# First layer's variance: the squares of centred tokens, in place of the squares of x less the squared mean

## The chip, the core and the metric

The kernel runs on one core of one Trainium2 chip. A core has five engines with queues of their own, which meet only at semaphores: TensorE (PE in the profile; its weight loads are PEld), VectorE (DVE), ScalarE (ACT), GpSimd (POOL) and SyncE (SP), which here only issues transfers. The metric is the device time of one execution in microseconds, lower is better; three runs of the kernel before gave 126.55, 126.73 and 127.25 us.

## What is computed

The input is 128 x 128 tokens of 32 channels, in fp32. Layer 0 is normalised over the channels, gated and multiplied along one of the token axes; layer 1 projects what comes out of it, gates it with a sum over a token axis and normalises again. The change lies in the first of the normalisations:

```python
def _layernorm(x, w, b):
    m = jnp.mean(x, axis=-1, keepdims=True)
    v = jnp.mean(jnp.square(x - m), axis=-1, keepdims=True)
    return (x - m) * jax.lax.rsqrt(v + EPS) * w + b
residual = pair_repr
x = _layernorm(pair_repr, ln1_w, ln1_b)
left = jax.nn.sigmoid(x @ left1) * (x @ left2)
right = jax.nn.sigmoid(x @ right1) * (x @ right2)
p = jnp.einsum('nsre,nkre->nske', left, right)
p = _layernorm(p, ln2_w, ln2_b)
g = jax.nn.sigmoid(jnp.einsum('nsrz,zy->nsry', x, gate))
q = jnp.einsum('nrse,ez->nsrz', p, out_w) * g
return residual + q
```

The second layer (left + eq projection, times the summed right projection, times a gate, projected out, residual, layer norm) isn't touched by the change.

## The kernel before

The 128 partitions hold one token axis, the free dimension the other one (128 positions s) times 32 channels. x arrives in eight transfers, the blocks of SUMS1 (L49): positions 0-8, 8-16, 16-32, 32-48, 48-64, 64-96, 96-112, 112-128, numbered b = 0 to 7. For each block the first layer norm takes these steps, on three engines:

- VectorE `add_x(b)` sums the channels (L545), `mean(b)` divides by 32 (L552) and writes minus the squared sum over 32 (L553).
- ScalarE `square1(b)` squares x itself (L381), waiting for nothing but the block's transfer. VectorE `add_squares(b)` sums the squares (L559), `difference` adds the two sums (L566), `variance1` clamps at zero (L573).
- ScalarE `root1_of` takes the root (L384), VectorE `inverse1` the reciprocal (L579). Roots are taken over the ranges of ROOTS1 (L50): as the blocks, but 6 and 7 together (root 6).
- GpSimd `centre(b)` subtracts the mean (L244), `normalise1(n)` multiplies with the reciprocal (L253), for turn n of TURNS (L51): two turns of 8 positions, then one of 16 for each of seven further chunks. VectorE does both itself for block 0 (L603, L611).

TensorE then transposes the normalised tokens (`transpose_xn(n)`, L841), ScalarE takes them out of PSUM with weight and bias (`affine1(n)`, L396) and, from chunk 2 on, also rounds them to fp32r (L400); GpSimd (chunks 2 and 3) or VectorE takes what the rounding left (L210). TensorE projects each chunk in two halves (`project_lr(c, h)`, half number j = 2c + h; L862 for chunks 0 and 1, L866 to L868 from chunk 2 on). The result of a half lies in one of three pairs of PSUM banks, so half j waits until VectorE has finished half j - 3. ScalarE takes the sigmoid of a half (`sigmoid_lr`, L409), VectorE multiplies (`multiply_lr`, L587).

Root and sigmoid lie in different tables of ScalarE. So all roots up to root 5 stand ahead of the first sigmoid in ScalarE's queue, and root 6 stands alone in the middle of the sigmoids, between two table loads. The order on each engine is written out by hand; each engine works through its list in that order, and a waiting instruction holds up all behind it.

When all 16 halves are through, TensorE multiplies left with right (L908), and the rest of layer 0 and layer 1 follow.

## Time and profile before

| | |
|---|---|
| median of 3 runs | 126.73 us (126.55 to 127.25) |
| span of the profiled execution | 125.2 us, some 1.5 us under the median (its own time is not given apart) |
| busy: PE / DVE / ACT / POOL | 100.3 / 96.3 / 77.4 / 72.8 us |
| first normalisation and the 16 halves | from the start to about 47 us |
| TensorE's granted clock, mean | 0.920 of full |

The span runs from the first to the last instruction. What lies around it isn't seen in the profile, and is taken to be the same for both kernels: the 1.5 us between span and median. The chain of waits is 51% TensorE, 18% VectorE and 15% ScalarE. TensorE's clock is granted in full or at half: the page's row for it reads 5 in the slices from about 9.5 to 19 us, 7 in two slices near 65 us, and 9 elsewhere.

### The profile page before, as it was taken

The numbers are of one execution on the slowest core, as the hardware profiler recorded it, in microseconds if no ns is written. First come the engines' busy times: TensorE is split into PE (matmuls) and PEld (weight loads), VectorE is DVE, ScalarE is ACT, GpSimd is POOL, SyncE is SP. The second block draws the span as 40 slices with busy tenths as digits, with TensorE's granted clock in tenths as the row PEclk, the third lists the DMA queues.
The fourth block names the chain that finished last, engine by engine and source line by source line (L and its number), as shares of the span: only waits on it lengthen the run. The fifth ranks groups of instructions, "written<-read, shape, count | busy, mean of one in ns | idle before, by whom it ended". The sixth has DMA issues, their size and how long they took to land.

```text
span 125.2 us, 1712 instructions
## 1 busy us (share of the span) xinstructions
PE 100.3 (80%) x526; PEld 74.6 (60%) x526; DVE 96.3 (77%) x227; ACT 77.4 (62%) x136; POOL 72.8 (58%) x78
## 2 busy tenths in 40 slices
PE   2937799498899996999749779999999999698000
PEld 2923254266577785994234338888977989597000
DVE  1569997399999975499999936384778989799920
ACT  2335366999995632999213994647599599761000
POOL 4086786757099500396073089758774596996700
PEclk9995558999999999999977999999999999999955
DMA  3999990000000000000000000000000005329796
GB/s 59 152 137 149 145 97 3 0 0 0 0 0 5 3 0 0 0 5 3 0 0 0 0 0 0 0 0 5 3 0 0 0 0 80 52 40 143 109 145 105
DMA packets 33324, 4.51 MB, mean 36 GB/s; under 512 B 33188, under 2 KB 33316, under 8 KB 33316
## 3 DMA queue, kind: packets, MB, share of 16 engines
q1 hardware_dynamic: 32000, 4.06, 26.3%
q10 hardware_dynamic: 1316, 0.35, 1.4%
q8 instruction: 4, 0.07, 0.2%
q14 instruction: 4, 0.03, 0.1%
HBM read 2.31 MB, written 2.10 MB: 35 GB/s over the span
## 4 chain that ended last, share of the span: by engine, by line
PE 51%; DVE 18%; ACT 15%; issue 6%; DMA 5%; SPq 0%; DVEq 0%; ACTq 0%
PE bank L862 6%; PE bank L866 5%; PE bank L997 5%; DMA x_tok<-in_x 5%; PE bank L868 4%; PE bank L867 4%; PE bank L1006 4%; PE bank L954 4%; ACT p_sb L450 3%; PE bank L968 3%; PE bank L841 3%; PE bank L971 3%; PE bank L969 3%; ACT sq L451 3%; DVE lr L778 3%
## 5 line engine op out<-in xcount | busy, mean ns | idle before, releaser
L587 DVE TENSOR_TENSOR lr<-bank,sig_lr 128x512 f32<-128x512 f32 x16 | 16.7, 1072 | 3.3 <-ACT sig_lr L409 3.2
L336 POOL TENSOR_TENSOR xn_low<-x1T,xn_high 128x512 fp32r<-128x512 f32 x8 | 11.1, 1381 | 12.2 <-ACT xn_high L472 12.2
L862 PE MATMUL bank<-lr_blk,xnT 128*128 128x512 f32 x16 | 11.5, 847 | 3.1 <-DVE lr L587 1.7
L328 POOL TENSOR_TENSOR t_tok<-p_sb,rstd 128x512 f32<-128x512 f32 x7 | 10.2, 1451 | 5.0 <-DVE rstd L735 4.9
L409 ACT ACTIVATE sig_lr<-bank 128x512 f32<-128x512 f32 x16 | 9.5, 594 | 4.7 <-PE bank L868 4.5
L866 PE MATMUL bank<-lr_high,xn_high 128*128 128x512 f32 x24 | 10.1, 421 | 1.2 <-issue 1.2
L352 POOL TENSOR_TENSOR sq<-lr,row_rep 128x512 f32<-128x512 f32 x7 | 9.8, 1398 | 2.0 <-DVE lr L781 2.0
L761 DVE SCALAR_TENSOR_TENSOR o_a<-bank,leq_bias,sig 128x512 f32<-128x512 f32 x8 | 6.0, 748 | 6.1 <-ACT sig L484 3.8
L253 POOL TENSOR_TENSOR xc<-xc,rstd 128x512 f32<-128x512 f32 (+1 forms) x8 | 7.9, 994 | 4.4 <-DVE rstd L579 4.4
L344 POOL TENSOR_TENSOR oT<-o_a,rsum 128x512 f32<-128x512 f32 x8 | 8.7, 1086 | 2.4 <-issue 1.8
L384 ACT ACTIVATE std<-st,eps 128x16 f32<-128x16 f32 (+4 forms) x14 | 4.4, 316 | 8.8 <-DVE st L767 4.3
L752 DVE SCALAR_TENSOR_TENSOR x1T<-bank,w_rep,u 128x128 f32<-128x128 f32 x32 | 9.3, 348 | 0.4
L868 PE MATMUL bank<-lr_high,xn_low 128*128 128x512 f32 x24 | 9.5, 396 | 0.0
L867 PE MATMUL bank<-lr_low,xn_high 128*128 128x512 f32 x24 | 9.5, 394 | 0.0
L244 POOL TENSOR_TENSOR xc<-x_tok,sums 128x512 f32<-128x512 f32 (+2 forms) x7 | 7.9, 1139 | 2.6 <-DVE sums L552 2.3
L1006 PEld LDWEIGHTS bank<-wout_blk,oT 128*128 128x128 f32 x64 | 8.2, 191 | 1.9 <-POOL oT L344 1.4
L1006 PE MATMUL bank<-wout_blk,oT 128*128 128x128 f32 x64 | 8.5, 276 | 1.0 <-POOL oT L344 1.0
L396 ACT ACTIVATE xnT<-bank,w_rep 128x512 f32<-128x512 f32 (+1 forms) x9 | 6.6, 729 | 3.9 <-PE bank L841 3.9
L954 PE MATMUL bank<-tT,out_blk 128*128 128x512 f32 x16 | 8.3, 598 | 0.8 <-DVE x1T L752 0.8
L997 PE MATMUL bank<-centre_blk,x1T 128*128 128x128 f32 x64 | 8.8, 280 | 0.0
L918 PE MATMUL bank<-xnT,gate_blk 128*128 128x512 f32 x16 | 8.4, 651 | 0.0
L472 ACT ACTIVATE xn_high<-x1T 128x512 fp32r<-128x512 f32 x8 | 5.1, 636 | 5.3 <-DVE x1T L752 5.3
(129 smaller groups left out, 279.5 us busy)
## 6 DMA issues: line engine op xcount, KB each, us to landing
out<-sq SPq DMA_DIRECT2D x7, 256.0 KB, 3.3
x_tok<-in_x SPq DMA_DIRECT2D x5, 256.0 KB, 6.4
x_tok<-in_x SPq DMA_DIRECT2D x1, 512.0 KB, 7.6
x_tok<-in_x SPq DMA_DIRECT2D x2, 128.0 KB, 4.2
w_rep<-in_weights ACTq DMA_DIRECT2D x1, 180.5 KB
out<-sq ACTq DMA_DIRECT2D x1, 128.0 KB, 4.5
out<-sq SPq DMA_DIRECT2D x1, 128.0 KB, 4.9
row_rep<-in_rows ACTq DMA_DIRECT2D x1, 32.0 KB, 5.4
```

What stands on the lines that cost most here:

```text
L328: nc.gpsimd.tensor_tensor(t_tok[:, c % 2], p_sb[:, :, s].rearrange("p e s -> p s e"), rstd[:, 1:2, s].rearrange("p a s -> p s a").to_broad ...
L336: nc.gpsimd.tensor_tensor(x1_low[:, c % 2], x1T[:, c % 3], x1_high[:, c % 2], ALU.subtract).then_inc(x1_low_ready, 1)
L352: nc.gpsimd.tensor_tensor(sq[:, s, :], yn[:, s, :], row_rep[:, 1:2, :].to_broadcast([P, SPC, CH]), ALU.add).then_inc(final, 1)
L409: nc.scalar.activation(sig_lr[:, j % 3].rearrange("p (s f) -> p s f", f=2 * CH), src[:, :, 0:2 * CH], ACT.Sigmoid).then_inc(lr_sig, 1)
L587: nc.vector.tensor_tensor(lr[:, :, s].rearrange("p f s -> p s f"), src[:, :, 2 * CH:4 * CH], sig_lr[:, j % 3].rearrange("p (s f) -> p s f" ...
L862: last = nc.tensor.matmul(bank[:, b], xnT[:, c, cols], lr_blk[:].rearrange("p g m c -> p (g m c)"), start=True, stop=True)
L866: nc.tensor.matmul(bank[:, b], xn_high[:, c % 3, cols], high, start=True, stop=False)
L867: nc.tensor.matmul(bank[:, b], xn_high[:, c % 3, cols], low, start=False, stop=False)
L868: last = nc.tensor.matmul(bank[:, b], xn_low[:, c % 3, cols], high, start=False, stop=True)
L954: nc.tensor.matmul(bank[:, Q], out0_blk[:], tT[:, c % 2], start=True, stop=True).then_inc(q_ps, 1)
L997: nc.tensor.matmul(bank[:, b, k], x1T[:, c % 3, k], centre_blk[:], start=j == 0, stop=False, skip_group_check=True)
L1006: last = nc.tensor.matmul(bank[:, b, k], oT[:, c % 2, k], wout_blk[:], start=False, stop=j == BLK - 1, skip_group_check=True)
```

## The change

ScalarE squares the centred tokens `xc` and no longer x. The sum of these squares over 32 is the variance, so that the squared mean, the difference and the clamp go: eight instructions of L553, seven of L566 and seven of L573 on VectorE, with their semaphores. The root reads the sum of squares. `square1(b)` now waits for the block's centring: on VectorE for block 0, on GpSimd for the others. The lists of ScalarE and VectorE are written anew; those of TensorE, GpSimd and SyncE stay as they are. A part of VectorE's list and what doesn't bear on the order is left out here:

```diff
--- before.py
+++ after.py
@@ -377,16 +377,20 @@
 
             def square1(b):
                 lo, hi = SUMS1[b]
-                act.wait_ge(x_in[b], 16)
-                nc.scalar.activation(sq[:, lo:hi, :], x_tok[:, lo:hi, :], ACT.Square).then_inc(squared1, 1)
+                if b < OWN_CENTRE:
+                    act.wait_ge(centre0, 1)
+                else:
+                    act.wait_ge(centred1_pool, b + 1 - OWN_CENTRE)
+                nc.scalar.activation(sq[:, lo:hi, :], xc[:, lo:hi, :], ACT.Square).then_inc(squared1, 1)
 
             def root(layer, lo, hi, done):
-                nc.scalar.activation(std[:, layer, lo:hi], st[:, layer, lo:hi], ACT.Sqrt, scale=1.0 / CH,
+                of = sums1[:, 2, lo:hi] if layer == 0 else st[:, layer, lo:hi]
+                nc.scalar.activation(std[:, layer, lo:hi], of, ACT.Sqrt, scale=1.0 / CH,
                                      bias=eps[:]).then_inc(done, 1)
 
             def root1_of(b):
                 lo, hi = ROOTS1[b]
-                act.wait_ge(var1, holding(SUMS1, hi - 1) + 1)
+                act.wait_ge(sumsq1, holding(SUMS1, hi - 1) + 1)
                 root(0, lo, hi, root1)
 
@@ -414,23 +418,22 @@
             square1(0)
-            square1(1)
             root1_of(0)
-            square1(2)
             act.wait_ge(w_in, 16)
             affine1(0)
+            square1(1)
             root1_of(1)
+            square1(2)
+            affine1(1)
+            root1_of(2)
             square1(3)
-            root1_of(2)
-            square1(4)
-            affine1(1)
             root1_of(3)
-            square1(5)
             act.wait_ge(lr_blk_ready, 1)
             nc.scalar.activation(lr_high[:], lr_blk[:], ACT.Copy).then_inc(lr_high_ready, 1)
             affine1(2)
+            square1(4)
             root1_of(4)
-            square1(6)
+            square1(5)
             root1_of(5)
             for c in range(CHUNKS):
                 sigmoid_lr(c, 0)
@@ -439,7 +442,8 @@
                 sigmoid_lr(c, 1)
-                if c == 0:
+                if c == 1:
+                    square1(6)
                     square1(7)
@@ -550,28 +554,11 @@
                 sums = sums1[:, 1, lo:hi]
                 dve.wait_ge(sum1, b + 1)
                 nc.vector.tensor_scalar(sums1[:, 0, lo:hi], sums, 1.0 / CH, None, ALU.mult).then_inc(mean1, 1)
-                nc.vector.scalar_tensor_tensor(out=sums1[:, 2, lo:hi], in0=sums, scalar=-1.0 / CH, in1=sums,
-                                               op0=ALU.mult, op1=ALU.mult).then_inc(minus1, 1)
 
             def add_squares(b):
                 lo, hi = SUMS1[b]
                 dve.wait_ge(squared1, b + 1)
-                nc.vector.tensor_reduce(sums1[:, 3, lo:hi], sq[:, lo:hi, :], AX.X, ALU.add).then_inc(sumsq1, 1)
-
-            def difference(first, last):
-
-                lo, hi = SUMS1[first][0], SUMS1[last][1]
-                dve.wait_ge(minus1, last + 1)
-                dve.wait_ge(sumsq1, last + 1)
-                nc.vector.tensor_tensor(st[:, 0, lo:hi], sums1[:, 3, lo:hi], sums1[:, 2, lo:hi],
-                                        ALU.add).then_inc(diff1, last + 1 - first)
-
-            def variance1(first, last):
-
-                lo, hi = SUMS1[first][0], SUMS1[last][1]
-                dve.wait_ge(diff1, last + 1)
-                nc.vector.tensor_scalar(st[:, 0, lo:hi], st[:, 0, lo:hi], 0.0, None,
-                                        ALU.max).then_inc(var1, last + 1 - first)
+                nc.vector.tensor_reduce(sums1[:, 2, lo:hi], sq[:, lo:hi, :], AX.X, ALU.add).then_inc(sumsq1, 1)
 
@@ -595,55 +582,43 @@
             add_x(0)
             mean(0)
-            add_squares(0)
-            difference(0, 0)
-            variance1(0, 0)
             lo, hi = SUMS1[0]
             dve.wait_ge(mean1, 1)
             nc.vector.tensor_tensor(xc[:, lo:hi, :], x_tok[:, lo:hi, :],
                                     sums1[:, 0:1, lo:hi].rearrange("p a s -> p s a").to_broadcast([P, hi - lo, CH]),
                                     ALU.subtract).then_inc(centre0, 1)
+            add_squares(0)
             add_x(1)
+            mean(1)
             inverse1(0)
-            mean(1)
             dve.wait_ge(centre0, 1)
             dve.wait_ge(rstd1, 1)
...
             inverse1(2)
-            mean(3)
+            add_x(4)
+            mean(4)
             add_squares(3)
-            add_x(4)
-            difference(3, 3)
-            mean(4)
-            variance1(3, 3)
+            inverse1(3)
+            add_x(5)
+            mean(5)
             add_squares(4)
-            inverse1(3)
-            difference(4, 4)
-            add_x(5)
-            variance1(4, 4)
-            mean(5)
+            inverse1(4)
             add_squares(5)
-            inverse1(4)
-            difference(5, 5)
             dve.wait_ge(lr_high_ready, 1)
-            variance1(5, 5)
             nc.vector.tensor_tensor(lr_low[:], lr_blk[:], lr_high[:], ALU.subtract).then_inc(lr_split, 1)
             inverse1(5)
             for c in range(CHUNKS):
@@ -660,8 +635,6 @@
                 if c == 1:
                     add_squares(6)
                     add_squares(7)
-                    difference(6, 7)
-                    variance1(6, 7)
```

On ScalarE, between the first affine step and the first sigmoid, the queue before is this (`sq` the squares, `std` the roots, `xnT` the affine steps, `lr_high` the weights' rounding; a `sq` of 1024 columns is block 5's, an `xnT` of 256 is turn 1's and one of 512 chunk 1's):

```order
L384 ACTIVATE std<-st,eps 128x8
L381 ACTIVATE sq<-x_tok 128x512
L384 ACTIVATE std<-st,eps 128x16
L381 ACTIVATE sq<-x_tok 128x512
L396 ACTIVATE xnT<-bank,w_rep 128x256
L384 ACTIVATE std<-st,eps 128x16
L381 ACTIVATE sq<-x_tok 128x1024
L430 ACTIVATE lr_high<-lr_blk 128x512
L396 ACTIVATE xnT<-bank,w_rep 128x512
L384 ACTIVATE std<-st,eps 128x16
L381 ACTIVATE sq<-x_tok 128x512
L384 ACTIVATE std<-st,eps 128x32
```

and after the change this:

```order
L388 ACTIVATE std<-sums,eps 128x8
L384 ACTIVATE sq<-xc 128x512
L400 ACTIVATE xnT<-bank,w_rep 128x256
L388 ACTIVATE std<-sums,eps 128x16
L384 ACTIVATE sq<-xc 128x512
L388 ACTIVATE std<-sums,eps 128x16
L432 ACTIVATE lr_high<-lr_blk 128x512
L400 ACTIVATE xnT<-bank,w_rep 128x512
L384 ACTIVATE sq<-xc 128x512
L388 ACTIVATE std<-sums,eps 128x16
L384 ACTIVATE sq<-xc 128x1024
L388 ACTIVATE std<-sums,eps 128x32
```

The squares of blocks 3, 4 and 5 have moved down: block 4's and block 5's stand behind the affine step of chunk 1, each right ahead of its own root, and root 2 stands behind the affine step of turn 1.

On VectorE, from root 3's reciprocal to root 5's, the queue before is this (`sums<-x_tok` is `add_x`, `sums<-sq` is `add_squares`, `sums<-sums` the mean or the squared mean, `rstd` the reciprocal):

```order
L579 RECIPROCAL rstd<-std 128x16
L566 TENSOR_TENSOR st<-sums 128x16
L545 TENSOR_REDUCE sums<-x_tok 128x32
L573 TENSOR_SCALAR st<-st 128x16
L552 TENSOR_SCALAR sums<-sums 128x32
L553 SCALAR_TENSOR_TENSOR sums<-sums 128x32
L559 TENSOR_REDUCE sums<-sq 128x32
L579 RECIPROCAL rstd<-std 128x16
L566 TENSOR_TENSOR st<-sums 128x32
L573 TENSOR_SCALAR st<-st 128x32
L647 TENSOR_TENSOR lr_low<-lr_blk,lr_high 128x512
L579 RECIPROCAL rstd<-std 128x32
```

and after the change this:

```order
L566 RECIPROCAL rstd<-std 128x16
L549 TENSOR_REDUCE sums<-x_tok 128x32
L556 TENSOR_SCALAR sums<-sums 128x32
L561 TENSOR_REDUCE sums<-sq 128x16
L566 RECIPROCAL rstd<-std 128x16
L561 TENSOR_REDUCE sums<-sq 128x32
L622 TENSOR_TENSOR lr_low<-lr_blk,lr_high 128x512
L566 RECIPROCAL rstd<-std 128x32
```

Five small instructions are gone, and the sum of block 4's squares has moved from ahead of root 3's reciprocal to behind block 5's mean.

On ScalarE, among the first sigmoids (`sig_lr`), the queue before is this (`xn_high` is the rounding of a chunk):

```order
L409 ACTIVATE sig_lr<-bank 128x512
L381 ACTIVATE sq<-x_tok 128x512
L409 ACTIVATE sig_lr<-bank 128x512
L396 ACTIVATE xnT<-bank,w_rep 128x512
L400 ACTIVATE xn_high<-xnT 128x512
L409 ACTIVATE sig_lr<-bank 128x512 x2
L396 ACTIVATE xnT<-bank,w_rep 128x512
```

and after the change this:

```order
L413 ACTIVATE sig_lr<-bank 128x512 x2
L400 ACTIVATE xnT<-bank,w_rep 128x512
L404 ACTIVATE xn_high<-xnT 128x512
L413 ACTIVATE sig_lr<-bank 128x512
L384 ACTIVATE sq<-xc 128x512 x2
L413 ACTIVATE sig_lr<-bank 128x512
L400 ACTIVATE xnT<-bank,w_rep 128x512
```

Both late squares (blocks 6 and 7) now stand between the sigmoids of halves 3 and 4. Before, block 6's stood ahead of all sigmoids and block 7's between those of halves 1 and 2.

## Rows read from the trace of the kernel before

**Rows 1.** Chain that ended last, in order of time: start us, us, what.

```profile
19.83 0.94 DVE st L573
...
20.79 0.32 ACT std L384
...
21.13 1.28 ACT L409
```

**Rows 2.** Groups of instructions by line, VectorE: xcount, busy us, mean ns, idle before.

```profile
L566 DVE TENSOR_TENSOR st<-sums 128x16 f32<-128x16 f32 (+2 forms) x7 | 2.3, 331 | 0.2
L573 DVE TENSOR_SCALAR st<-st 128x16 f32<-128x16 f32 (+2 forms) x7 | 2.2, 316 | 0.2
...
L553 DVE SCALAR_TENSOR_TENSOR sums<-sums 128x16 f32<-128x16 f32 (+2 forms) x8 | 1.3, 166 | 0.0
```

**Rows 3.** Timeline of VectorE: start us, us, engine line op out<-in, [idle before <-releaser].

```profile
7.11 0.42 DVE L545 TENSOR_REDUCE sums<-x_tok 128x8 f32<-128x256 f32 x1 [1.58 <-DMA x_tok<-in_x]
...
7.87 0.94 DVE L552 TENSOR_SCALAR sums<-sums 128x8 f32<-128x8 f32 x1
...
8.80 0.41 DVE L611 TENSOR_TENSOR xc<-xc,rstd 128x256 f32<-128x256 f32 x1
...
12.65 0.24 DVE L579 RECIPROCAL rstd<-std 128x16 f32<-128x16 f32 x1
...
12.93 0.68 DVE L559 TENSOR_REDUCE sums<-sq 128x16 f32<-128x512 f32 x1
...
16.26 1.21 DVE L545 TENSOR_REDUCE sums<-x_tok 128x32 f32<-128x1024 f32 x1
...
31.44 1.03 DVE L587 TENSOR_TENSOR lr<-bank,sig_lr 128x512 f32<-128x512 f32 x1
...
35.22 1.07 DVE L587 TENSOR_TENSOR lr<-bank,sig_lr 128x512 f32<-128x512 f32 x1
```

**Rows 4.** Timeline of GpSimd (POOL), same columns.

```profile
7.51 1.26 POOL L272 TENSOR_TENSOR lr_blk<-w_rep,mask 128x512 f32<-128x512 f32 x1
8.89 0.80 POOL L244 TENSOR_TENSOR xc<-x_tok,sums 128x256 f32<-128x256 f32 x1
...
11.43 0.61 POOL L253 TENSOR_TENSOR xc<-xc,rstd 128x256 f32<-128x256 f32 x1
...
17.77 1.91 POOL L244 TENSOR_TENSOR xc<-x_tok,sums 128x1024 f32<-128x1024 f32 x1 [0.45 <-DVE sums L552]
19.67 1.05 POOL L253 TENSOR_TENSOR xc<-xc,rstd 128x512 f32<-128x512 f32 x1
...
28.67 2.08 POOL L244 TENSOR_TENSOR xc<-x_tok,sums 128x512 f32<-128x512 f32 x2
```

**Rows 5.** Timeline of ScalarE (ACT), same columns.

```profile
14.75 0.56 ACT L396 ACTIVATE xnT<-bank,w_rep 128x256 f32<-128x256 f32 x1 [1.81 <-PE bank L841]
...
15.59 1.04 ACT L381 ACTIVATE sq<-x_tok 128x1024 f32<-128x1024 f32 x1
...
22.43 0.60 ACT L409 ACTIVATE sig_lr<-bank 128x512 f32<-128x512 f32 x1
...
24.74 0.62 ACT L381 ACTIVATE sq<-x_tok 128x512 f32<-128x512 f32 x1
...
28.22 0.78 ACT L396 ACTIVATE xnT<-bank,w_rep 128x512 f32<-128x512 f32 x1
...
33.19 0.60 ACT L409 ACTIVATE sig_lr<-bank 128x512 f32<-128x512 f32 x1
```

**Rows 6.** Timeline of TensorE (PE), same columns.

```profile
24.24 1.96 PE L862 MATMUL bank<-lr_blk,xnT 128*128 128x512 f32 x4 [1.69 <-DVE lr L587]
...
64.28 1.11 PE L943 MATMUL bank<-ident,t_tok 128*128 128x128 f32 x4 [2.54 <-DVE t_tok L737]
```

**Rows 7.** Stretches: busy us of each engine (instructions), PE clock, DMA share, GB/s.

```profile
38.00:47.00 9.00, 9.00 (x44) 7.33 (x43) 8.06 (x9) 4.79 (x8) 4.44 (x10) 1.00 0.01 3
64.00:66.00 2.00, 1.72 (x5) 1.25 (x6) 2.00 (x3) 0.57 (x1) 1.83 (x2) 0.54 0.00 0
```

More of the change, by code:

```diff
@@ L139, in pair_layers @@
         st = sb("st", [P, 3, P])
-        sums1 = sb("sums1", [P, 4, P])
+        sums1 = sb("sums1", [P, 3, P])
         std = sb("std", [P, 3, P])
@@ L175, in pair_layers @@
         wout_centred = sem("wout_centred")
-        sum1, minus1, sumsq1, diff1 = sem("sum1"), sem("minus1"), sem("sumsq1"), sem("diff1")
+        sum1, sumsq1 = sem("sum1"), sem("sumsq1")
         mean1, centred1_pool, squared1 = sem("mean1"), sem("centred1_pool"), sem("squared1")
-        var1, root1, rstd1 = sem("var1"), sem("root1"), sem("rstd1")
+        root1, rstd1 = sem("root1"), sem("rstd1")
         xn_ready, xn_pool = sem("xn_ready"), sem("xn_pool")
@@ L613, in _ @@
                                     ALU.mult).then_inc(xn_ready, 1)
+            add_x(2)
+            mean(2)
             add_squares(1)
-            add_x(2)
-            difference(1, 1)
-            mean(2)
-            variance1(1, 1)
+            inverse1(1)
+            add_x(3)
+            mean(3)
             add_squares(2)
-            inverse1(1)
-            difference(2, 2)
             dve.wait_ge(wprod, 1)
@@ L625, in _ @@
                                     mask[:], ALU.mult).then_inc(out0_ready, 1)
-            variance1(2, 2)
             nc.vector.tensor_copy(q_bias[:], bank[:, 7, CH:CH + 1]).then_inc(out0_ready, 1)
-            add_x(3)
             inverse1(2)
-            mean(3)
+            add_x(4)
+            mean(4)
             add_squares(3)
-            add_x(4)
-            difference(3, 3)
-            mean(4)
-            variance1(3, 3)
+            inverse1(3)
+            add_x(5)
+            mean(5)
             add_squares(4)
-            inverse1(3)
-            difference(4, 4)
-            add_x(5)
-            variance1(4, 4)
-            mean(5)
+            inverse1(4)
             add_squares(5)
-            inverse1(4)
-            difference(5, 5)
             dve.wait_ge(lr_high_ready, 1)
-            variance1(5, 5)
             nc.vector.tensor_tensor(lr_low[:], lr_blk[:], lr_high[:], ALU.subtract).then_inc(lr_split, 1)
```

## The prediction

> **What bounds the kernel now.** I read the chain of waits first, then the timelines of the engines over the first 47 us, where all of the change lies, then the stretches with the clock. From 38 to 47 us TensorE is busy all of the time at the full clock [rows 7]: these are the last projections, and what comes behind them (left times right, then layer 1) is untouched by the change and starts when they end. So the question is by how much the end of the projections moves. Before that dense part TensorE waits for others. The last large wait is the 1.69 us before 24.24, for the multiplication of half 0 on VectorE [rows 6]. It stands behind the first sigmoid at 22.43 [rows 5], that behind the table load at 21.13, and that behind root 5 at 20.79, which waits for the clamp at 19.83 [rows 1]. In short: the first sigmoid can't start until all roots up to root 5 are taken, and what sets root 5 sets the time.
>
> **What is removed.** 22 small VectorE instructions with 2.3 + 2.2 + 1.3 = 5.8 us of busy time [rows 2]. Little of it is on the chain. The part that counts is the clamp ahead of root 5: 0.94 us, where its fellows of L573 have a mean of 316 ns with it counted in [rows 1, 2]. It runs from 19.83 to 20.77 while GpSimd works from 19.67 to 20.72 on L253 [rows 4], and ends with it. In the same way the mean at 7.87 takes 0.94 us and ends at 8.81, when GpSimd's L272 (7.51 to 8.77) is done [rows 3, 4]. So the small VectorE instructions that scale or clamp are held by a running GpSimd instruction; the change takes away some that can be held and keeps the means. Were nothing else changed, root 5 could come about 1.3 us earlier, by clamp and difference (0.94 + 0.33) [rows 1, 2].
>
> **What is added: a wait for the centring.** The square of a block no longer waits for the transfer alone but for transfer, sum, mean and GpSimd's centring. Behind the waiting square on ScalarE stand roots, affine steps and sigmoids; for these wait VectorE's reciprocals, GpSimd's normalising and TensorE. I follow it from the row at 7.11.
>
> *Block 0.* The sum of block 1 ends at 7.11 + 0.42 = 7.53 [rows 3]. Its mean now stands ahead of the reciprocal, meets L272 and ends when the one before did, 8.81. Only then come the reciprocal (at most 0.24) and the multiplication of block 0, which was at 8.80 [rows 3]; now not before 8.97. GpSimd's centring of block 1 starts at 8.89. In the trace the multiplication was first, and that centring took 0.80 us, where a multiplication of the same size took 0.61 [rows 4]: the one that comes second waits for the first. Now GpSimd is first, until 8.89 + 0.61 = 9.50, so TensorE's first transposition is later by 9.50 - 8.80 = 0.70. If the two don't hold each other, by 0.17. I take 0.70, the direction that the 0.80 speaks for.
>
> The Trainium skill, page "SBUF — State Buffer", section "SBUF: two separate sides", says that VectorE and GpSimd share a pair of ports under an exclusive lock, which an operation of VectorE with two SBUF inputs needs too, and that the loser waits for the whole instruction. By it the start is 0.70 later, without it 0.17; the trace agrees with it in the 0.80 us.
>
> *Root 2 to root 5.* TensorE's first projections start with that transposition, so the affine step of turn 1, 14.75 to 15.31 [rows 5], ends at 16.01. Before, root 2 was taken ahead of it; now it stands behind: 16.01 + 0.32 (root 5's duration [rows 1]) = 16.33, its reciprocal 0.24 [rows 3] to about 16.6, normalising of turn 2 on GpSimd 1.05 [rows 4], 16.7 to 17.7. VectorE sums block 4 beside it (0.68 [rows 3]), and the mean of block 4 is held until 17.75. Sum of block 3's squares 0.68: 18.45. Root 3: 18.8. Reciprocal: 19.1. Sum of block 5, 1.21 [rows 3]: 20.3; GpSimd's normalising of turn 3 ends at about the same time. Mean 0.17 (the mean of L553, of the same size [rows 2]): 20.5. Centring of block 5, 1.91 [rows 4]: 22.45. In the trace the same centring started at 17.77, and nobody but the normalising waited for it. Square of block 5, 1.04 [rows 5]: 23.5. Sum of squares, 1024 columns again 1.21: 24.75. Root 5: 25.1. The table load starts at 25.1 in place of 21.13 [rows 1]: **+4.0 us**, in spite of the 1.3 us that clamp and difference give back. The work of block 4 lies beside this: its square, sum and root fit in the 1.91 us of centring. TensorE has no cover for it, since it already waited at 24.24: half 3 starts at 28.2.
>
> *The late squares.* Block 7's square goes from between the sigmoids of halves 1 and 2, so what follows there comes 0.6 earlier (0.62 [rows 5]), net +3.4. GpSimd centres blocks 6 and 7 only behind two roundings' remainders, at 28.67 for 2.08 us [rows 4]: now at 32.1 until 34.15. The square of block 7 ends at 34.8, and only then the sigmoid of half 4. The affine step behind that, 28.22 before [rows 5], is at 34.8 + 0.6 = 35.4: +7.2. From there to the sigmoid of half 6 ScalarE has affine step, rounding, sigmoid, two table loads and root 6, which took 33.19 - 28.22 = 4.97 [rows 5]; so 40.4, and its end 41.0. In the trace ScalarE was ahead of VectorE here, which is the slack: VectorE took half 4 only at 31.44 and half 6 at 35.22 [rows 3]. Half 6 is now at 41.0: +5.8. TensorE needs that for half 9, the start of its dense part, and from then on nothing gives it back [rows 7]. So the sum is **+4.0 to the first sigmoid and +1.8 more from the late squares**. It charges every handover in full; and without the hold at block 0 it is 5.3. I take +5.4.
>
> The profiled span is 125.2; with 5.4 it is 130.6. What lies around the span is the 1.5 us by which the median of 126.73 exceeds it, so 132.1 for the median.
>
> **The clock.** TensorE will be nearly idle from about 23.3 (24.24 - 1.69 + 0.70 [rows 6]) to 28.2. After an idle time of 2.54 us before 64.28 [rows 6] the clock was granted at 0.54 over the next two us [rows 7], so to 1.2 GHz for nearly all of them. I expect the same here, but at no price: halves 3 to 6 are then slower while the late squares hold up half 7 anyhow. It costs from zero to the 1.9 us that two page slices of 3.13 us at 7 tenths make, if the clock falls again in the wait for half 6 at 41 and is half while TensorE is dense.
>
> **Rivals.**
> 1. *Half of it is hidden.* The late squares cost nothing beyond the first shift, because VectorE's own backlog (half 4 at 31.44 although its sigmoid had ended some 3 us before [rows 3, 5]) takes up the wait. For it: that slack. Against: root 6 stands between two table loads behind those squares, and the sigmoid of half 6 had no such slack. Then +3.4 to +4.0; with a mean of block 1 that slips in ahead of L272 (7.53 against 7.51, a close race) down to +3.2. Time 130.3, between 129.9 and 130.7.
> 2. *The clock falls in the dense part.* +5.4 + 1.9 at most; with 1.7, 133.8. For it: the drop at 64 us after only 2.54 us of idling, and new waits at halves 7 and 9. Against: these waits are shorter, some 1 to 2 us each. The Trainium skill, page "TensorE: Matmul & The Clock Gate", section "HAM oscillation — how this bites in real kernels", says that an array that waits throttles again and starts its next batch cold; by that rule the time is this rival's, and the 64 us rows agree.
> 3. *Not slower.* One mechanism: clamp and difference ahead of root 5 were the true last wait, and the centring of block 5 is done by the time ScalarE comes to its square. Then root 5 is 1.3 us earlier and the time is 125.4. It decides if the centring of block 5 ends before 19.7, one square (1.04) and one sum (1.21), less the 1.3, ahead of root 5 at 20.79. In the trace it ended at 17.77 + 1.91 = 19.68 [rows 4], so just in time; that is what speaks for it. Against: the new order puts root 2, normalising, root 3 and the mean of block 5 in a row behind the affine step of turn 1, and that puts the centring at 22.45.
> That the change doesn't do what it says can be left out: the instructions are gone from the queue.
>
> **How the numbers follow.** Forecast +5.4 with its own range of 131.2 to 133.0: chance 0.50. Rival 1: 0.27. Rival 2: 0.17. Rival 3: 0.04, of which half within no change; another 0.02 for what I don't see. About 0.5% is what a measurement of this kernel can tell from no change. Faster 0.02, same 0.03, slower 0.95. The time is the likeliest case's, 132.1; the range, from rival 1's lower end to rival 2's with the clock nearly in full, is 129.9 to 134.4.
>
> **What would show it.** The first sigmoid's table load near 25 us, and ahead of it ScalarE idle for GpSimd's centring of block 5. The normalising multiplication of block 0 on VectorE starting with or after the end of GpSimd's first centring. ScalarE idle before the two squares of blocks 6 and 7. TensorE's last projection near 52.4 in place of 47. It is wrong if the table load comes before 24, if VectorE takes half 6 before 39.5, or if anything behind the projections is shorter or longer than before by over 0.5 us.

## The result

The changed kernel takes 132.17 us (median of 4 runs, 131.63 to 132.44); the kernel before, in the same comparison, 126.66. The ratio on record is 1.0409, 95% interval 1.0371 to 1.0448: slower by 4% (the quotient of the two medians, 1.0435, lies within it). The forecast was 132.1, in a range of 129.9 to 134.4. The profiled execution is the fastest of the four: 131.63 us, with a span of 129.8, so 1.8 us lie around the span. That is so in every execution whose span is on record, of both kernels (1.75 to 1.86 us), and not 1.5 us as was taken for the kernel before. Its page, cut to the span, the busy times and the clock:

```profile
span 129.8 us, 1681 instructions
...
PE 101.6 (78%) x526; PEld 75.2 (58%) x526; DVE 93.7 (72%) x205; ACT 77.3 (60%) x136; POOL 72.5 (56%) x78
...
PEclk9995559958999999999999959999999999999755
```

VectorE's busy time fell from 96.3 to 93.7 us, with 22 instructions less. The span rose by 4.6 us all the same: the instructions that went were not what the end waited for.

### The profile page after: what moved, and what is told of

Read it like the earlier page. It is cut to its first block, busy times and chain, and to the rows that moved or that the text cites. A ratio compares the mean times of both kernels' runs of the same rounds, so it can differ in the third digit from the quotient of the medians.

```text
span 129.8 us, 1681 instructions
## 1 busy us (share of the span) xinstructions
PE 101.6 (78%) x526; PEld 75.2 (58%) x526; DVE 93.7 (72%) x205; ACT 77.3 (60%) x136; POOL 72.5 (56%) x78
## 4 chain that ended last, share of the span: by engine, by line
PE 50%; DVE 24%; ACT 9%; issue 6%; DMA 4%; POOL 2%; DVEq 0%; SPq 0%; ACTq 0%; POOLq 0%
PE bank L835 6%; PE bank L927 6%; DVE acc_p L667 5%; PE bank L970 5%; PE bank L839 4%; DMA x_tok<-in_x 4%; PE bank L979 4%; PE bank L841 4%; PE bank L840 4%; PE bank L941 3%; PE bank L944 3%; PE bank L942 3%; PE bank L900 3%; DVE lr L751 3%; ACT sig_lr L413 2%
## 5 line engine op out<-in xcount | busy, mean ns | idle before, releaser
L835 PE MATMUL bank<-lr_blk,xnT 128*128 128x512 f32 x16 | 13.1, 952 | 5.6 <-DVE lr L574 4.1
L413 ACT ACTIVATE sig_lr<-bank 128x512 f32<-128x512 f32 x16 | 9.3, 592 | 5.0 <-PE bank L841 3.9
L927 PE MATMUL bank<-tT,out_blk 128*128 128x512 f32 x16 | 9.2, 660 | 2.2 <-DVE x1T L725 2.2
L835 PEld LDWEIGHTS bank<-lr_blk,xnT 128*128 128x128 f32 x16 | 4.1, 290 | 8.9 <-ACT xnT L400 5.4
L814 PEld LDWEIGHTS bank<-ident,xc 128*128 128x128 f32 x32 | 4.5, 161 | 6.9 <-POOL xc L253 3.8
L244 POOL TENSOR_TENSOR xc<-x_tok,sums 128x512 f32<-128x512 f32 (+2 forms) x7 | 7.9, 1135 | 1.0 <-DVE sums L556 0.7
L718 DVE SCALAR_TENSOR_TENSOR u<-bank,q_bias,gT 128x512 f32<-128x512 f32 x8 | 5.9, 739 | 3.6 <-PE bank L927 3.6
```

The lines of the kernel that those rows point to most:

```text
L413: nc.scalar.activation(sig_lr[:, j % 3].rearrange("p (s f) -> p s f", f=2 * CH), src[:, :, 0:2 * CH], ACT.Sigmoid).then_inc(lr_sig, 1)
L835: last = nc.tensor.matmul(bank[:, b], xnT[:, c, cols], lr_blk[:].rearrange("p g m c -> p (g m c)"), start=True, stop=True)
L927: nc.tensor.matmul(bank[:, Q], out0_blk[:], tT[:, c % 2], start=True, stop=True).then_inc(q_ps, 1)
```

## The profile after

The chain that ended last, over the stretch up to TensorE's half 3 (start us, us, what):

```profile
14.28 0.56 ACT xnT L400
...
17.78 1.05 POOL xc L253
...
19.07 1.92 POOL xc L244
...
21.02 1.06 ACT sq L384
...
22.11 1.23 DVE sums L561
...
23.36 0.32 ACT std L388
...
23.70 1.28 ACT L413
...
25.62 1.05 DVE lr L574
...
26.80 3.47 PE bank L835 x4
```

This answers to [rows 1]. Root 5 is at 23.36 (20.79 before) and the table load at 23.70 (21.13): +2.57. Ahead of it no clamp stands any longer, but what the prediction put there: the affine step of turn 1, GpSimd's normalising of turn 3 and centring of block 5 (L244, 1.92), that block's square (1.06) and its sum (1.23). TensorE's half 3, which is released by the multiplication at 25.62, starts at 26.80, +2.56 against [rows 6].

VectorE in the same kernel, at block 1's sum and mean, block 0's multiplication, and half 6's multiplication, which answers to 35.22 in [rows 3]:

```profile
6.62 0.42 DVE L549 TENSOR_REDUCE sums<-x_tok 128x8 f32<-128x256 f32 x1 [1.24 <-DMA x_tok<-in_x]
7.08 0.18 DVE L556 TENSOR_SCALAR sums<-sums 128x8 f32<-128x8 f32 x1
...
7.47 1.29 DVE L596 TENSOR_TENSOR xc<-xc,rstd 128x256 f32<-128x256 f32 x1
...
39.30 1.04 DVE L574 TENSOR_TENSOR lr<-bank,sig_lr 128x512 f32<-128x512 f32 x1 [0.40 <-ACT sig_lr L413]
```

and GpSimd, at L272, the centring of block 1 and those of blocks 6 and 7 [rows 4]:

```profile
7.19 1.29 POOL L272 TENSOR_TENSOR lr_blk<-w_rep,mask 128x512 f32<-128x512 f32 x1
8.44 0.80 POOL L244 TENSOR_TENSOR xc<-x_tok,sums 128x256 f32<-128x256 f32 x1
...
30.69 2.06 POOL L244 TENSOR_TENSOR xc<-x_tok,sums 128x512 f32<-128x512 f32 x2
```

Block 1 landed 0.5 us earlier than in the trace of before (6.62, 7.11), so its mean (7.08) came just ahead of L272 (7.19). What L272 then held was the multiplication of block 0: 1.29 us in place of 0.41, and GpSimd's centring at 8.44 took 0.80 once more, as the second of the two.

ScalarE between the sigmoids of halves 3 and 6 (L384 the two late squares, L413 the sigmoids of halves 3, 4 and 6) [rows 5]:

```profile
30.31 0.60 ACT L413 ACTIVATE sig_lr<-bank 128x512 f32<-128x512 f32 x1 [1.09 <-PE bank L835]
31.77 0.63 ACT L384 ACTIVATE sq<-xc 128x512 f32<-128x512 f32 x1 [0.86 <-POOL xc L244]
32.78 0.63 ACT L384 ACTIVATE sq<-xc 128x512 f32<-128x512 f32 x1 [0.38 <-POOL xc L244]
33.32 0.58 ACT L413 ACTIVATE sig_lr<-bank 128x512 f32<-128x512 f32 x1
...
38.67 0.60 ACT L413 ACTIVATE sig_lr<-bank 128x512 f32<-128x512 f32 x1
```

It waits 0.86 and 0.38 us for GpSimd's centrings; the sigmoid of half 6 is at 38.67 (33.19 before). VectorE takes half 6 at 39.30, 4.08 later than before: 1.5 us have come on top of the 2.57. TensorE's first transposition, and its start on left times right:

```profile
8.82 0.44 PE L814 MATMUL bank<-ident,xc 128*128 128x128 f32 x2 [1.16 <-DVE xc L596]
...
53.22 7.41 PE L881 MATMUL bank<-lr 128*128 128x128 f32 x64 [1.18 <-DVE lr L574]
```

The first is at 8.82, earlier than before (9.27), by about as much as the transfer was. The second is at 53.22, 48.73 before: +4.49. From there to the end of the span it is 76.6 us, 76.5 before, so all of the loss lies ahead of it. The stretches of half 3 and of the last projections [rows 7] (busy us of each engine, then TensorE's clock):

```profile
26.00:28.00 2.00, 1.20 (x2) 0.71 (x3) 1.22 (x2) 1.97 (x5) 1.32 (x2) 0.61 0.00 0
28.00:30.00 2.00, 2.00 (x4) 0.80 (x3) 2.00 (x4) 1.19 (x2) 0.96 (x2) 0.53 0.00 0
46.00:52.00 6.00, 6.00 (x30) 4.91 (x28) 4.92 (x6) 2.79 (x6) 0.00 (x0) 1.00 0.01 1
```

The clock was at half, 1.2 GHz, for most of 26 to 30 us, behind TensorE's wait of 4.11 us for the multiplication of half 0.

## The experiments

Each ratio is to the kernel before on the same chip, with its 95% interval. Medians are of four to ten executions, the trace is of one of them, and its time can lie up to 0.8 us from the median; where the two say different things, both are given.

**Blocks 6 and 7 by the old method.** In the changed kernel:

```diff
             square1(5)
+            square_x(6)
             root1_of(5)
...
-                if c == 1:
-                    square1(6)
-                    square1(7)
+                if c == 0:
+                    square_x(7)
```

where `square_x` squares x and waits for the transfer; block 6 and 7's squared mean, difference and clamp are back.

> The changed kernel, but blocks 6 and 7 by the method of before: squares of x (block 6's ahead of root 5, block 7's between the sigmoids of halves 1 and 2), squared mean, difference and clamp. The theory of the prediction: the late squares cost 1.5 us (VectorE took half 6 4.08 us later than before while the first sigmoid was 2.57 later), so this run should be 1.2 to 2.0 us faster than the changed kernel, near 130.5 us, with half 6 at most 3 us later than before. Rival: VectorE's and TensorE's backlog would have cost the same without them (TensorE ran half 3 at half clock): within 0.5 us of the changed kernel, near 132.

Measured: 131.11 us, ratio 1.0309 (1.0248 to 1.0369). That is 1.0% under the changed kernel, 1.3 us, at the lower end of what was expected. Half 6, which was to come at most 3 us later than before, is a miss in this trace: VectorE took it at 39.27, 4.05 later, as in the changed kernel. Part of that is the start, since the table load is 0.74 later than there (24.44, 23.70), and part is TensorE's clock. Its ScalarE, at the table load and the sigmoids of halves 3, 4 and 6, and TensorE's half 3:

```profile
24.44 1.28 ACT L422 ACT_TABLE_LOAD   x1
...
31.33 0.60 ACT L422 ACTIVATE sig_lr<-bank 128x512 f32<-128x512 f32 x1 [0.85 <-PE bank L856]
33.24 0.60 ACT L422 ACTIVATE sig_lr<-bank 128x512 f32<-128x512 f32 x1 [1.31 <-PE bank L862]
...
38.63 0.60 ACT L422 ACTIVATE sig_lr<-bank 128x512 f32<-128x512 f32 x1
```

```profile
27.55 3.75 PE L856 MATMUL bank<-lr_blk,xnT 128*128 128x512 f32 x4 [4.11 <-DVE lr L587]
```

The late squares are gone, but the sigmoid of half 4 now waits 1.31 us for TensorE, whose half 3 takes 3.75 us at half clock (1.96 in [rows 6]). The two costs lie side by side; the run named "Both" below takes them apart. This trace also has the hold at block 0 as the prediction described it. VectorE's mean of block 1 and multiplication of block 0, then GpSimd's L273 (L272 of before) and its centring of block 1:

```profile
7.17 1.11 DVE L565 TENSOR_SCALAR sums<-sums 128x8 f32<-128x8 f32 x1
...
8.49 0.76 DVE L609 TENSOR_TENSOR xc<-xc,rstd 128x256 f32<-128x256 f32 x1
```

```profile
6.98 1.28 POOL L273 TENSOR_TENSOR lr_blk<-w_rep,mask 128x512 f32<-128x512 f32 x1
8.36 0.61 POOL L245 TENSOR_TENSOR xc<-x_tok,sums 128x256 f32<-128x256 f32 x1
```

The mean runs 1.11 us, to the end of L273, and the multiplication 0.76, ending 0.28 us after the centring. In these traces the form goes with which is first, the mean or L272, and the two are 0.1 to 0.2 us apart. Of the six traces in which VectorE's list has this order, four have this form and two have the other, the changed kernel's and that of the run with TensorE kept at work.

**The same in the kernel before.** Blocks 6 and 7 by the new method, all else as before:

```diff
             root1_of(4)
-            square1(6)
             root1_of(5)
...
-                if c == 0:
-                    square1(7)
+                if c == 1:
+                    square_centred(6)
+                    square_centred(7)
```

> The kernel before, but only blocks 6 and 7 by the new method (squares of centred tokens, both between the sigmoids of halves 3 and 4). First sigmoid at 22 to 22.5 us as before in every theory. If the late squares cost by themselves: 1.3 to 2.0 us slower than before, 128.0 to 128.7. If they are hidden by VectorE's backlog when nothing else is late: within 0.5 us of before.

Measured: 128.61 us, 1.0115 (1.0082 to 1.0148), as expected if they cost by themselves: 1.5 us. ScalarE at the first sigmoid, the two squares and the sigmoid of half 6:

```profile
22.07 0.60 ACT L418 ACTIVATE sig_lr<-bank 128x512 f32<-128x512 f32 x1
...
28.86 0.63 ACT L386 ACTIVATE sq<-xc 128x512 f32<-128x512 f32 x1 [1.38 <-POOL xc L244]
29.87 0.63 ACT L386 ACTIVATE sq<-xc 128x512 f32<-128x512 f32 x1 [0.38 <-POOL xc L244]
...
35.76 0.60 ACT L418 ACTIVATE sig_lr<-bank 128x512 f32<-128x512 f32 x1
```

The first sigmoid is 0.36 earlier than before (22.43), that of half 6 is 2.57 later (33.19), behind waits of 1.38 and 0.38 us for the centring. TensorE's half 3 took 2.96 us in this trace, so the clock had fallen here too; the table below says what that is worth.

**The new order without the new waits.** The changed kernel's lists, with squares of x:

```diff
-                if b < OWN_CENTRE:
-                    act.wait_ge(centre0, 1)
-                else:
-                    act.wait_ge(centred1_pool, b + 1 - OWN_CENTRE)
-                nc.scalar.activation(sq[:, lo:hi, :], xc[:, lo:hi, :], ACT.Square).then_inc(squared1, 1)
+                act.wait_ge(x_in[b], 16)
+                nc.scalar.activation(sq[:, lo:hi, :], x_tok[:, lo:hi, :], ACT.Square).then_inc(squared1, 1)
```

and the squared mean, the difference and the clamp back, behind each mean and each sum of squares.

> The changed kernel's order of ScalarE's and VectorE's lists, but with squares of x, which wait for the transfer alone, and squared mean, difference and clamp right behind each sum of squares. If the wait for GpSimd's centring is what costs (prediction): the table load comes before 23 us, and the time is 128.0 to 130.0. If it is the order in which the squares of blocks 4 to 7 were put behind affine steps and sigmoids: first table load near 23.7 or later, time 130.5 to 132.5, as the changed kernel, or slower, since the small instructions are there too.

Measured: 132.55 us, 1.0437 (1.0395 to 1.0479): no faster than the changed kernel, though no square waits for a centring. ScalarE's square of block 5 and table load, and VectorE's difference of block 4:

```profile
22.97 1.04 ACT L382 ACTIVATE sq<-x_tok 128x1024 f32<-128x1024 f32 x1
...
26.15 1.28 ACT L410 ACT_TABLE_LOAD   x1
```

```profile
21.44 1.07 DVE L567 TENSOR_TENSOR st<-sums 128x16 f32<-128x16 f32 x1
```

The square of block 5 can't run before 22.97, since it stands behind root 4, and that waits for the difference of block 4, which ran 1.07 us. That the time comes out nearly the same is chance: the table load is 2.45 us later than in the changed kernel (23.70), and left times right only 0.99 (54.21, 53.22), since blocks 6 and 7 wait for no centring. So the run isn't a clean measure of the order.

The rows allow an estimate. The affine step of turn 1 starts 0.72 us later than in the changed kernel (15.00, 14.28). From the end of a sum of squares to the root it lets go, this run has 0.72 us for block 3, 1.42 for block 4 and 0.55 for block 5; the changed kernel, with no difference and no clamp between them, has 0.03 or 0.04 each time. That is 2.6 us of small instructions. Without them and from the same start the table load would be near 26.15 - 0.72 - 2.6 = 22.8. So of the 2.57 us by which the changed kernel's table load is later than 21.13, some 0.9 are the wait (its square of block 5 waits 0.80 us for the centring), and 1.7 are the order, less what the missing small instructions give back.

**Block 0 early.** In the changed kernel:

```diff
             add_squares(0)
-            add_x(1)
-            mean(1)
             inverse1(0)
...
+            add_x(1)
+            mean(1)
```

(the lines left out multiply block 0).

> The changed kernel, but VectorE takes block 0's reciprocal and multiplication ahead of block 1's sum and mean. Root 0 ends at 5.7 us in the changed kernel, so the multiplication can run at 6, before GpSimd works. If the hold of that multiplication by GpSimd's instruction delays TensorE's start: first transposition near 7.7 in place of 8.8, everything behind it as much earlier, 1 to 2 us faster than the changed kernel, 130 to 131. If the roots behind set the first sigmoid and not TensorE's start: within 0.5 us of it.

Measured: 129.84 us, 1.0212 (1.0174 to 1.0250), so 2.0% under the changed kernel, a little more than expected. ScalarE's table load:

```profile
22.30 1.28 ACT L413 ACT_TABLE_LOAD   x1
```

It is 1.40 us earlier than in the changed kernel, and TensorE's first transposition (7.77) 1.05 us: TensorE's start is on the path to root 5, by the affine step of turn 1. The trace shows 1.4 us of the 2.0%, which are 2.5 us. The changed kernel's own trace has an early start, 8.82; in the four traces with the mean held it is 9.29 to 9.58.

**Block 0 early in the kernel before**, with root 0 ahead of block 1's square as well (VectorE's part is as in the run above, and left out here).

```diff
             square1(0)
-            square1(1)
             root1_of(0)
+            square1(1)
```

> The kernel before, but root 0 ahead of block 1's square on ScalarE, and block 0's reciprocal and multiplication ahead of block 1's sum on VectorE. The same move made the changed kernel some 2.4 us faster (1.0409 to 1.0212 of the kernel before). If it works through TensorE's start alone: first transposition near 7.7 in place of 9.3, and 0.8 to 2 us faster than before, near 125.5. If what it saved there was the hold of that multiplication by GpSimd, which the kernel before hasn't got (its multiplication took 0.41 us), within 0.5 us of before.

Measured: 126.56 us, 0.9971 (0.9951 to 0.9990). TensorE's first transposition and half 3:

```profile
7.62 0.42 PE L841 MATMUL bank<-ident,xc 128*128 128x128 f32 x2
...
23.19 3.10 PE L862 MATMUL bank<-lr_blk,xnT 128*128 128x512 f32 x4 [2.81 <-DVE lr L587]
```

The first is 1.65 us earlier than in the kernel before (9.27), and the table load, at 20.09, 1.04; yet only 0.3% are won. That lies in the range of the second expectation, but not by its reason, since the start did move. TensorE waits 2.81 us, and half 3 takes 3.10 us in place of 1.96 [rows 6], the clock having fallen on the way. Left times right starts 0.57 us earlier than before (48.16, 48.73), so about half of the 1.04 us is lost behind the first sigmoid.

**TensorE kept at work** in the changed kernel's wait:

```diff
-                for s in range(lo, hi, GRP):
...
+                for _ in range(9 if n == 4 else 1):
+                    for s in range(lo, hi, GRP):
```

> The changed kernel, with the transposition of chunk 3 done nine times over (same values to the same place), so that TensorE is at work in its wait for half 0's multiplication. The clock should stay at full (2.4 GHz) and half 3 take 2.0 us in place of 3.5. The prediction says that the fall of the clock costs nothing, since the late squares hold up half 4 anyway: within 0.5 us of the changed kernel (1.036 to 1.046 of before). Rival, the clock costs what it shows: 1.3 to 1.7 us faster, 1.029 or less of before.

Measured: 132.10 us, 1.0395 (1.0355 to 1.0436), no change against 1.0409. Half 3:

```profile
27.23 1.95 PE L836 MATMUL bank<-lr_blk,xnT 128*128 128x512 f32 x4 [0.63 <-DVE lr L574]
```

Its 1.95 us, as in [rows 6], show that the clock stayed full. So in the changed kernel the fall of the clock costs nothing that can be measured, as predicted.

**Both.** Blocks 6 and 7 by the old method, with the repeated transpositions.

```diff
+            square_x(6)
...
+                for _ in range(9 if n == 4 else 1):
```

> The run with blocks 6 and 7 by the old method, with the repeated transpositions as well. There TensorE's half 3 took 3.75 us and the sigmoid of half 4 waited 1.3 us for TensorE, so the clock was the bound that took the late squares' place. Then this run is 1.0 to 1.8 us faster than that one (1.0309 of before): 1.017 to 1.023. If the clock is hidden here too: within 0.5 us of it, 1.027 to 1.035.

Measured: 129.96 us, 1.0215 (1.0169 to 1.0261), with half 3 in 1.96 us. So taking away the late squares alone gives 1.0%, the slow clock alone nothing, and the two together 1.9%: the clock hides behind the squares. Against the same kernel without the repeats (1.0309) the intervals of the times overlap by a little. The traces say more. The stretch from the start of VectorE's multiplication of half 0 to the start of left times right leaves out how early an execution got going (all in us):

| | late squares | half 3 takes | half 0 multiplied | left times right | between |
|---|---|---|---|---|---|
| the kernel before | no | 1.96 | 23.06 | 48.73 | 25.67 |
| both (this run) | no | 1.96 | 26.65 | 52.22 | 25.57 |
| kernel before, block 0 early | no | 3.10 | 22.01 | 48.16 | 26.15 |
| blocks 6 and 7 by the old method | no | 3.75 | 26.36 | 53.19 | 26.83 |
| the changed kernel | yes | 3.47 | 25.62 | 53.22 | 27.60 |
| TensorE kept at work | yes | 1.95 | 26.03 | 53.62 | 27.59 |
| late squares in the kernel before | yes | 2.96 | 22.70 | 50.31 | 27.61 |

The slow clock costs up to 1.26 us where the squares are early (26.83, 25.57) and nothing where they are late (27.60, 27.59). The late squares cost 1.9 to 2.0 us (27.6 against 25.67 and 25.57). The changed kernel's loss in its trace is thus 2.56 us ahead of half 0's multiplication and 1.93 behind it.

**Another order with the new waits.** ScalarE's list alone, in the changed kernel:

```diff
             square1(2)
-            affine1(1)
             root1_of(2)
             square1(3)
+            affine1(1)
             root1_of(3)
+            square1(4)
...
             affine1(2)
-            square1(4)
             root1_of(4)
```

> The changed kernel, with another order of ScalarE's list alone: root 2 and block 3's square ahead of the affine step of turn 1, block 4's square ahead of the rounding of the weights. All waits for the centring stay. The run with the new order but without these waits was as slow as the changed kernel, so the order should be the cause of the late first sigmoid: table load at 21 to 22 us in place of 23.7, and 1.5 to 2.5 us faster than the changed kernel, 1.021 to 1.030 of before. If the wait for the centring is the cause after all: table load after 23, within 0.5 us of the changed kernel.

Measured: 130.00 us, 1.0237 (1.0215 to 1.0259), so 1.7% under the changed kernel, 2.2 us. The table load, expected at 21 to 22 us, is at 22.36. ScalarE's squares of blocks 3, 4 and 5 and its table load:

```profile
13.93 0.63 ACT L384 ACTIVATE sq<-xc 128x512 f32<-128x512 f32 x1 [0.23 <-POOL xc L244]
...
16.30 0.63 ACT L384 ACTIVATE sq<-xc 128x512 f32<-128x512 f32 x1 [0.23 <-POOL xc L244]
...
19.68 1.06 ACT L384 ACTIVATE sq<-xc 128x1024 f32<-128x1024 f32 x1
...
22.36 1.28 ACT L413 ACT_TABLE_LOAD   x1
```

The squares of blocks 3 and 4 wait 0.23 us for their centring, block 5's not at all, and the table load is 1.34 us earlier than in the changed kernel's trace although TensorE's first transposition came 0.5 us later here than there (9.34, 8.82).

**The clamp left out**, in the kernel before. The result differs only where rounding makes a variance negative by more than eps.

```diff
                 nc.vector.tensor_tensor(st[:, 0, lo:hi], sums1[:, 3, lo:hi], sums1[:, 2, lo:hi],
-                                        ALU.add).then_inc(diff1, last + 1 - first)
+                                        ALU.add).then_inc(var1, last + 1 - first)
```

> The kernel before without the clamp of the variance at zero (seven small VectorE instructions left out; eps is still added ahead of the root, so that the result differs only where rounding makes a variance negative by more than eps). This is the part of the change that takes small instructions off the chain and moves nothing. Root 5 waited for a clamp of 0.94 us. If that is its price: first sigmoid 0.7 to 1.1 us earlier, 0.5 to 1.0 us faster than before, 0.992 to 0.996 of it. Rival: the difference ahead of it is held by the same GpSimd instruction and then takes the clamp's place, or TensorE falls to half clock in what is left: within 0.3%, 0.997 to 1.003.

Measured: 125.62 us, 0.9869 (0.9836 to 0.9903), more than expected (the quotient of the medians is 0.9890, near the interval's upper end). VectorE at the difference of block 5, and ScalarE's table load:

```profile
19.72 0.13 DVE L566 TENSOR_TENSOR st<-sums 128x32 f32<-128x32 f32 x1
```

```profile
20.26 1.28 ACT L409 ACT_TABLE_LOAD   x1
```

The difference takes 0.13 us and the table load comes 0.87 us earlier than in [rows 1]. Left times right starts at 47.60, 1.13 us earlier than before (48.73), so another 0.26 us come behind the first sigmoid. What the 1.3% hold beyond these 1.1 us no trace shows. This part of the change is a gain by itself; the moved squares outweigh it.

**Clamp and block 0.** The last two edits to the kernel before, together.

```diff
-            square1(1)
             root1_of(0)
+            square1(1)
...
-                                        ALU.add).then_inc(diff1, last + 1 - first)
+                                        ALU.add).then_inc(var1, last + 1 - first)
```

> The kernel before with block 0 taken early (0.9971 of before by itself) and without the clamp. If the two add: first sigmoid near 20.5 us, 0.988 to 0.994. If TensorE's clock in its wait for half 0 eats the gain (it ran half 3 in 3.1 in place of 2.0 us with block 0 early): 0.995 to 1.0, with half 3 at over 2.5 us.

Measured: 125.04 us, 0.9847 (0.9824 to 0.9869). It had half 3 in 1.95 us, so the clock wasn't lost. The gain is larger than expected because the missing clamp gave more than expected: 0.9869 times 0.9971 is 0.984. The intervals overlap with the run before it, and what block 0 adds is not settled.

**The new variance at its best, as far as these runs go**: blocks 0 to 5 by the new method, ScalarE's list reordered, block 0 early, blocks 6 and 7 by the old method, TensorE kept at work.

```diff
             root1_of(2)
             square1(3)
+            affine1(1)
             root1_of(3)
+            square1(4)
...
+            square_x(6)
             root1_of(5)
...
+                for _ in range(9 if n == 4 else 1):
```

> The new variance for blocks 0 to 5 with all that the runs found: ScalarE's list reordered, block 0 early, blocks 6 and 7 by the old method, and TensorE kept at work in its wait. Against the changed kernel these gave -1.7%, -2.0%, and -1.9% for the last two together. If the centring's wait is cheap in itself and the loss lay in order and clock: 0.995 to 1.008 of before. If the centring of block 5 (1.9 us on GpSimd ahead of its square) is a floor of its own: table load no earlier than 21.5 us and 1.008 to 1.02.

Measured: 127.27 us, 1.0019 (1.0003 to 1.0035), the first of the two expectations; but the table load, at 21.41, is where the second had it. VectorE's sum of block 5, and ScalarE's square of block 5 and table load:

```profile
15.27 1.22 DVE L558 TENSOR_REDUCE sums<-x_tok 128x32 f32<-128x1024 f32 x1 [0.26 <-DMA x_tok<-in_x]
```

```profile
18.73 1.06 ACT L385 ACTIVATE sq<-xc 128x1024 f32<-128x1024 f32 x1 [1.10 <-POOL xc L245]
...
21.41 1.28 ACT L422 ACT_TABLE_LOAD   x1
```

The wait for the centring of block 5 is 1.10 us here: with order and clock out of the way it becomes the bound. The sum at 15.27 had waited for the block's transfer. From there the sum (1.22), the mean (0.18), GpSimd's centring (1.91, at 16.78), the square (1.06), its sum (1.22) and root 5 (0.32) follow one another up to 21.41 with gaps of under 0.1 us. With these blocks, these transfers and this method no order of the lists would bring the table load much ahead of 21.4; a smaller block 5, or part of its centring on another engine, was not tried. The loss of 4% is undone, but the new variance is no gain: the kernel before with block 0 early is at 0.9971, with its table load at 20.09.

**The best version**: the kernel before with block 0 early, no clamp, and five rounds of the transposition of chunk 3.

```diff
+                for _ in range(5 if n == 4 else 1):
```

> The kernel before with block 0 early, no clamp, and the transposition of chunk 3 done five times over, to keep TensorE's clock. If the clock is what eats the gain: half 3 in 2.0 us and 0.980 to 0.990 of before, faster than the same without the repeats by 0.5 us or more. If not: within 0.3% of that one.

Measured: 124.69 us, 0.9822 (0.9798 to 0.9846), faster than both kernels. TensorE's half 3 and the start of left times right (48.73 before):

```profile
22.40 1.88 PE L860 MATMUL bank<-lr_blk,xnT 128*128 128x512 f32 x4
...
46.32 7.41 PE L906 MATMUL bank<-lr 128*128 128x128 f32 x64 [1.17 <-DVE lr L584]
```

Against the run without the repeats (0.9847) it is no measurable difference, and half 3 was at full clock there too.

## Why the prediction came out, and where it didn't

**The size and the place.** The median rose by 5.5 us, 5.4 were forecast; the ratio of 1.0409 makes it 5.2. The profiled span rose by 4.6 only, and it is what the steps speak of. The difference is in which executions were profiled: with 1.8 us around a span of 125.2 the one before took about 127.0 us (an estimate), 0.3 over its median, and the one after was 0.5 under its. So the steps forecast too much, 5.8 charged in full and 5.4 taken, where 4.5 came, and that the median agrees is in part luck. The place was right: nothing changed behind the projections (76.6 and 76.5 us).

**Root 2 to root 5.** Forecast +4.0 for the table load, measured +2.57; it was to be wrong "if the table load comes before 24", and it came at 23.70. 1.15 us of the 1.43 that are missing are the step at block 0: +0.70 forecast, -0.45 measured at the first transposition (8.82 against 9.27). Of these 1.15 us, 0.49 are that block 1 landed earlier in this trace, which is a matter of the execution and not of the kernel. The other 0.66 are that the mean slipped in ahead of L272, a race that the prediction named in its first rival. The multiplication was held all the same (1.29 us), by the instruction ahead of the one forecast. In four other traces, as in that of blocks 6 and 7 by the old method, mean and multiplication were held as forecast, 1.11 and 0.76 us, and TensorE started at 9.31. But there too the step cost less than 0.70: from the start of block 1's sum to the end of the multiplication it is 2.54 us (6.71 to 9.25), and 2.10 in the kernel before (7.11 to 9.21).

The Trainium skill's page "SBUF — State Buffer", section "SBUF: two separate sides", has the loser wait for the whole instruction; the trace agrees, the multiplication at 7.47 ended at 8.76, 0.28 after L272's end at 8.48.

**The wait or the order.** The prediction's heading for the loss was the wait for the centring. The runs say that up to the first sigmoid it was more the order of the lists. The waits in another order of ScalarE's list gave 1.7% back (1.0237), and VectorE's block 0 ahead of block 1 gave 2.0% (1.0212). The order without the waits was no faster (1.0437); with its small instructions taken off, the estimate above leaves some 0.9 us for the wait. The split between order and wait is thus an estimate; no run has the order with neither. The working had the order in it, root 2 behind the affine step and block 5's square behind root 4, but did not set it apart from the wait. The wait is what stays when the order is mended (1.10 us ahead of block 5's square, 1.0019).

**The late squares.** Forecast +1.8, measured 4.08 - 2.57 = 1.5 at half 6, and 1.5 us (1.0115) by themselves in the kernel before. By its own second sign the prediction was to be wrong if half 6 came before 39.5; it was forecast at 41.0 and came at 39.30, 1.4 of the 1.7 us by the first shift. So two of its three signs of being wrong came up, both by the size of the first shift. That ScalarE's two table loads leave no slack there was right, so the first rival (hidden in VectorE's backlog) falls. Another 0.4 us came behind half 6 (TensorE starts half 10 at 42.41, before at 37.94).

**The clock.** It fell as forecast, at no price as forecast: 1.0395 with the clock kept. The second rival, a fall in the dense part, didn't come about: 1.00 from 46 to 52 us. What the prediction did not say is that the clock stands right behind the late squares: take these away and the slow half 3 bounds, for up to 1.26 us.

**Not slower.** The third rival falls: the centring of block 5 ended at 20.98, not before 19.7. Its bound was also worked out with a wrong sign. Square and sum (1.04 + 1.21) still come between the centring and root 5, so for root 5 not to be later than 20.79 the centring had to end by 18.5, and for the whole 1.3 us of gain by 17.2; the 19.68 of the trace before was not just in time. But its gain is real where nothing else moves, 1.3% without the clamp.

## What to carry to other kernels

Fewer instructions on an engine are worth what the chain pays for them; here seven clamps were worth 1.3%, and the whole change, which moved the squares behind other work in an in-order queue and gave them waits of their own, still lost 4%. When an added wait comes with a new order, test order and wait apart: the same order without the wait, and the wait in another order. Two costs that lie side by side hide each other: here the slow clock was free while the squares were late, and taking the squares away alone gave less than they cost.

## What the runs showed of the hardware

A small VectorE instruction of 0.17 us took up to 1.31 us while GpSimd worked (the mean at 7.43 in the changed kernel with block 0 early; 1.11 in the rows above), and a multiplication of 0.41 up to 1.29. A sum of squares at 9.13 in the kernel before, beside GpSimd's centring at 8.89, kept its 0.41. TensorE's clock fell to half behind a wait of 4.11 us and also in one of 2.81; it stayed full behind the kernel before's 1.69 us, and when the same transposition was repeated through the wait.
